# L0 prologue of a four-layer fused kernel: a new order of loads, key and value products, norms and key sums

## Chip, cores and metric

The kernel runs on 1 core of one Trainium2 chip. Time is device microseconds of one launch, median of several runs. On this core the engines work side by side: PE (TensorE: matmuls, PEld its weight loads), DVE (VectorE), ACT (ScalarE), POOL (GpSimd) and SP (SyncE, which issues the DMAs). Each takes its own list of instructions in order; semaphores tie them together.

## The reference, cut to what matters

```python
x = x + jnp.tanh(g_xattn[0]) * _L0_xattn_ref(_layernorm(x), ctx_4096, Wq, Wk, Wv, Wo)   # 16 heads of 96, 4 KV heads
x = x + jnp.tanh(g_ffn[0])   * _L0_ffn_ref(_layernorm(x), ...)                          # base + top-2 LoRA experts
x = x + jnp.tanh(g_xattn[1]) * _L1_xattn_ref(_layernorm(x), ctx_4096, ctx_4096)         # linear attention
x = x + jnp.tanh(g_ffn[1])   * _L1_ffn_ref(_layernorm(x), ...)
...                                                                                      # L2 and L3 alike, with rope
```

In L0, keys and values come from `concat([context, latents])`: `k = hidden @ Wk.T`, `v = hidden @ Wv.T`, while `q = layernorm(x) @ Wq.T`. In L1, `kh = softmax(kh, axis=1)` and `kvs = einsum('bnhd,bnhe->bhde', kh, vh)` depend on the context alone, so they can be worked out at any time: these are the "key sums". x is 8 batches of 128 tokens by 512, the context as well.

## The kernel before, in words

One core holds all of x (`x`), its normed and transposed form (`xt_hi`, `xt_lo`) and the transposed context (`ct_hi`, `ct_lo`) in SBUF. Each fp32 operand is split into a rounded part `_hi` and a rest `_lo`, and every product is a `triple` of three matmuls (lines 440 to 442). A part `_hi` is a cast on ACT; the rest is a subtraction, on DVE for what lies in PSUM and for the context, on POOL for weights.

Work on weights: SP loads a tile into one of five slots of `raw` (`load_tile`, line 458), ACT casts it (`weight_head`, L2437), POOL takes the rest (`weight_tail`, L3219) and counts `w_done` up by one. Tile n counts in its place in the list, so the waits of PE are on the number of tiles done.

The L0 attention is done in 4 groups of heads. A group's projections ("fillers") are `K`, `W` (values, before they are turned), `Q`, and `V` (the turn of `W`), the ones with n = 0 from the context (`ct_*`), those of `Q` and with n = 1 from the tokens (`xt_*`). Each takes half of the tokens: 12 matmuls of 512 columns, `V` 4 transposes. A filler is named by its place (b, k); ACT (`head`) and DVE (`evacuate`) bring its result from PSUM to SBUF. The first 11 of group 0 are the prologue; after it come `three_groups` and the rest, in an order that is written out by hand for each engine. The first work of that part is `scores(0, 0)` on PE, L2518 on ACT.

Before the 11 fillers, the kernel does eight norms one after another: DVE statistics (`norm_stats`, L1424 to L1429), POOL the power of -0.5 (`norm_rstd`, L3211), DVE the normed rows (`norm_rows`, L1437), PE four transposes (`norm_transpose`, L582), ACT the cast (`norm_head`, L2423), DVE the rest (`norm_tail`, L1451). Only then are the context's four chunks cast (ACT L3183, DVE L2398), and then the five weight tiles of group 0. ACT's first work is the tanh of the gates (L3176), which waits for their load.

The key sums are one step for each of 8 batches, `l1_keys`, dealt out one before each filler: DVE the maximum of the context rows (L1898), ACT the exponentials (L2805), PE four transposes (L975, "turn"), ACT a cast (L2813), DVE the rest (L1903), PE twelve matmuls of 128 columns ("key products"), DVE three small operations (L1908 to L1911).

SP issues the loads in this order: constants, x (8), gates and `b_thr`, the transposed context (4 of 512 KB), four weight tiles, the context rows (8), the fifth weight tile, a bias row, the output weights.

## Time and profile before

| | |
|---|---|
| median of 3 runs | 1801.08 us (1800.53 to 1801.22) |
| the profiled execution's own time | 1802.1 us |
| its span, first to last instruction | 1800.3 us |
| PE busy | 1754.0 us, 97% of the span |
| DVE, ACT, POOL busy | 1213.5, 859.0, 969.2 us |

PE is the engine that is nearly always busy. The time around the span is 1.8 us in the profiled execution. Rows of the trace give a start, a duration, the engine, the line, what is written and read, and in brackets how long the engine had been idle and what ended that.

### The profile page before, as it was taken

How to read it: one execution, taken by the hardware profiler on the slowest of the kernel's cores; microseconds unless marked ns; L12 is line 12 of the kernel's file. 1: busy time of each engine (PE TensorE's matmuls, PEld its weight loads, DVE VectorE, ACT ScalarE, POOL GpSimd, SP SyncE). 2: the span in 40 equal slices, each digit the busy share in tenths (PEclk: the TensorE clock that was granted, in tenths of full speed). 3: DMA queues.
4: the chain of work that ended last, by engine and by line, in shares of the span. 5: the costliest groups of instructions: out<-in, count | busy, mean ns of one | idle time of the engine just before them, and what ended most of it. 6: DMA issues, size and time to landing. Idle time of an engine off the chain costs nothing.

```text
span 1800.3 us, 27501 instructions
## 1 busy us (share of the span) xinstructions
PE 1754.0 (97%) x8776; PEld 1438.7 (80%) x8776; DVE 1213.5 (67%) x2204; ACT 859.0 (48%) x2451; POOL 969.2 (54%) x806
## 2 busy tenths in 40 slices
PE   4999999999999999999999999999999999999999
PEld 3788888776878888888888877878888888888887
DVE  5566566688876666666666675766666666666685
ACT  4466666553554444444444453344444444444451
POOL 3032322266575656656566563575675756757561
PEclk9999999999999999999999998999999999999999
DMA  5010100020111101101011110110110101101101
GB/s 208 6 34 21 30 24 16 21 91 12 59 42 30 47 12 52 35 29 47 17 51 36 29 34 25 41 48 19 51 35 23 47 24 46 36 22 47 31 18 48
DMA packets 36853, 69.47 MB, mean 39 GB/s; under 512 B 4362, under 2 KB 5130, under 8 KB 36658
## 3 DMA queue, kind: packets, MB, share of 16 engines
q1 hardware_dynamic: 36786, 68.61, 12.6%
q8 instruction: 37, 0.61, 0.1%
q14 instruction: 30, 0.25, 0.0%
HBM read 66.50 MB, written 2.10 MB: 38 GB/s over the span
## 4 chain that ended last, share of the span: by engine, by line
PE 91%; DVE 4%; issue 2%; ACT 2%; POOL 1%; DMA 1%; SPq 0%; POOLq 0%; ACTq 0%; DVEq 0%
PE ps L440 27%; PE ps L442 26%; PE ps L441 26%; PE ps L671 4%; PE ps L652 3%; PE ps L582 1%; PE ps L613 1%; DVE negmax L1522 1%; DMA bthr<-in_b_thr 0%; POOL probs L3268 0%; POOL rope_a L3250 0%; DVE pt_loL L1544 0%; DVE ot_lo L1555 0%; ACT probs L2518 0%; DVE ot_lo L1550 0%
## 5 line engine op out<-in xcount | busy, mean ns | idle before, releaser
L3268 POOL TENSOR_TENSOR probs<-probs,rsums 128x512 f32<-128x512 f32 (+1 forms) x160 | 194.8, 1218 | 281.4 <-DVE rsums L1540 281.2
L3250 POOL TENSOR_TENSOR rope_a<-rope_a,rope_b 128x512 f32<-128x512 f32 x160 | 206.9, 1293 | 155.0 <-DVE rope_b L1515 154.8
L440 PE MATMUL ps<-wo_hiL,ot_hi 128*128 128x512 f32 x608 | 248.8, 409 | 3.0 <-DVE ot_lo L1555 2.2
L440 PE MATMUL ps<-xt_hi,wq_hiL 128*128 128x512 f32 x608 | 242.6, 399 | 0.2
L442 PE MATMUL ps<-wo_hiL,ot_lo 128*128 128x512 f32 x608 | 241.5, 397 | 0.0
L441 PE MATMUL ps<-wo_loL,ot_hi 128*128 128x512 f32 x608 | 241.3, 397 | 0.0
L442 PE MATMUL ps<-xt_hi,wq_loL 128*128 128x512 f32 x608 | 238.0, 391 | 0.0
L441 PE MATMUL ps<-xt_lo,wq_hiL 128*128 128x512 f32 x608 | 236.9, 390 | 0.0
L2518 ACT ACTIVATE probs<-ps,negmax 128x128 f32<-128x128 f32 x512 | 182.1, 373 | 88.3 <-DVE negmax L1522 88.2
L2535 ACT CAST ot_hi<-ps 128x512 fp32r<-128x512 f32 (+1 forms) x160 | 90.7, 567 | 257.0 <-PE ps L442 256.6
L3262 POOL TENSOR_TENSOR q_loL<-rope_a,q_hiL 128x512 fp32r<-128x512 f32 x128 | 164.5, 1294 | 28.1 <-ACT q_hiL L2505 28.1
L3219 POOL TENSOR_TENSOR wq_loL<-raw,wq_hiL 128x512 fp32r<-128x512 f32 x76 | 100.0, 1317 | 125.0 <-ACT wq_hiL L2437 125.0
L1561 DVE SCALAR_TENSOR_TENSOR x<-ps,tg,x 128x512 f32<-128x512 f32 x160 | 119.0, 743 | 67.9 <-PE ps L442 66.4
L1522 DVE TENSOR_REDUCE negmax<-ps 128x4 f32<-128x512 f32 (+1 forms) x160 | 126.7, 792 | 53.2 <-PE ps L652 40.5
L1544 DVE TENSOR_TENSOR pt_loL<-ps,pt_hiL 128x512 fp32r<-128x512 f32 (+1 forms) x160 | 126.9, 793 | 41.3 <-ACT pt_hiL L2528 39.9
L2528 ACT CAST pt_hiL<-ps 128x512 fp32r<-128x512 f32 (+1 forms) x160 | 108.0, 675 | 74.7 <-PE ps L671 63.8
L440 PEld LDWEIGHTS ps<-wo_hiL,ot_hi 128*128 128x128 f32 x608 | 115.1, 189 | 33.7 <-issue 5.5
L1550 DVE TENSOR_TENSOR ot_lo<-ps,ot_hi 128x512 fp32r<-128x512 f32 (+1 forms) x160 | 105.8, 661 | 49.7 <-ACT ot_hi L2539 24.2
L442 PEld LDWEIGHTS ps<-wo_hiL,ot_lo 128*128 128x128 f32 x608 | 114.9, 189 | 27.7
L3219 POOL TENSOR_TENSOR wo_loL<-raw,wo_hiL 128x512 fp32r<-128x512 f32 x76 | 97.6, 1295 | 68.8 <-ACT wo_hiL L2437 68.7
L442 PEld LDWEIGHTS ps<-xt_hi,wq_loL 128*128 128x128 f32 x608 | 114.1, 188 | 24.8
L441 PEld LDWEIGHTS ps<-wo_loL,ot_hi 128*128 128x128 f32 x608 | 115.2, 190 | 23.3
(231 smaller groups left out, 4267.0 us busy)
## 6 DMA issues: line engine op xcount, KB each, us to landing
raw<-in_L_proj SPq DMA_DIRECT2D x108, 256.0 KB, 2.6
raw<-in_L_out SPq DMA_DIRECT2D x76, 256.0 KB, 2.6
raw<-in_F_w SPq DMA_DIRECT2D x16, 256.0 KB, 2.7
x<-in_x SPq DMA_DIRECT2D x8, 256.0 KB, 4.3
ct_raw<-in_ctx_t SPq DMA_DIRECT2D x4, 512.0 KB, 7.6
cn_raw<-in_ctx SPq DMA_DIRECT2D x8, 256.0 KB, 8.1
out<-x SPq DMA_DIRECT2D x8, 256.0 KB, 2.0
raw<-in_L_kv SPq DMA_DIRECT2D x6, 256.0 KB, 2.9
```

What stands on the lines that cost most here:

```text
L440: pe.matmul(dst, l_hi, r_hi, start=start, stop=False)
L441: pe.matmul(dst, l_hi, r_lo, start=False, stop=False)
L442: return pe.matmul(dst, l_lo, r_hi, start=False, stop=stop)
L1522: v.tensor_reduce(negmax[:, b % 2], sc, X_AXIS, ALU.max, negate=True).then_inc(L.s_smax, 1)
L1544: v.tensor_tensor(L.pt_lo[:], ps[:, T_BANK:T_BANK + L.sources, :], L.pt_hi[:], ALU.subtract).then_inc(L.s_pt, 1)
L1561: v.scalar_tensor_tensor(out=x[:, b], in0=ps[:, Y_BANK, :], scalar=tg[:, L.gate:L.gate + 1], in1=x[:, b], op0=ALU.mult, op1=ALU.add).then_ ...
L2518: e = act.activation(probs[:, row:row + L.keys], ps[:, bank + at_ // 512, at_ % 512:at_ % 512 + L.keys], ACT.Exp, bias=offset[:, b % 2, h: ...
L2528: act.copy(L.pt_hi[:], ps[:, T_BANK:T_BANK + L.sources, :]).then_inc(L.s_pt_head, 1)
L3219: gp.tensor_tensor(lo, raw[0:parts, k % RAW, 0:cols], hi, ALU.subtract).then_inc(w_done, 1)
L3250: gp.tensor_tensor(rope_a[:, a], rope_a[:, a], rope_b[:], ALU.add).then_inc(L.s_rsum, 1)
L3262: gp.tensor_tensor(lo, rope_a[:, a], hi, ALU.subtract).then_inc(L.s_qk, 1)
L3268: gp.tensor_tensor(pv, pv, rsums[:, b % 2].unsqueeze(2).to_broadcast([P, GH, L.keys]), ALU.mult).then_inc(L.s_p, 1)
```

## The change

The L0 prologue is written as one list per engine, the function `prologue(a0)` of each. The context is loaded first, in halves of four batches (`ct_in[0]`, `ct_in[1]`), and the gates last. ACT casts a half in two pieces (`context_head(0..3)`); DVE takes the rest of the first half (`ct_done`), POOL that of the second (`context_tail`, `ct_rest`). The normed rows move from DVE to ACT (`norm_rows` there, L2432, an activation with a scale and a bias), for which DVE computes a bias for each batch (`norm_shift`, L1444). The fillers come in the order PRO_TWO, weight tiles in the order K, W, Q0, Q1, Q2. The step `l1_keys` is taken apart into `key_max`, `key_exps`, `key_turn`, `key_head`, `key_tail`, `key_products` and `key_sums`, each put into the lists by itself. A filler waits for the norms of its own half only. The norms use PSUM banks 6 and 7 in place of 0 and 1. `head(7, 1)` of ACT moves from `three_groups` into the list. No work is added but the eight `norm_shift`; the context's two halves of casts are as large as the four chunks were.

```diff
@@ module level @@
+PRO_TWO = [(3, 0), (4, 1), (3, 1), (5, 0), (4, 0), (5, 1), (6, 0), (6, 1), (6, 2), (7, 0), (7, 1)]
-NORM_BANK = {"A0": 0, "F0": 0, "F1": 2, "A2": 2, "F2": 0, "A3": 2, "F3": 0}
+NORM_BANK = {"A0": 6, "F0": 0, "F1": 2, "A2": 2, "F2": 0, "A3": 2, "F3": 0}
...
-        self.prologue = PRO_ROPE if rope else [(b, k) for b in range(3, 8) for k in range(len(self.fill[b]))]
-        self.pro_weights = PRO_WEIGHTS if rope else WEIGHT_ORDER
-        self.pro_tiles = PRO_TILES if rope else list(range(self.proj_tiles))
+        self.prologue = PRO_ROPE if rope else PRO_TWO
+        self.pro_weights = PRO_WEIGHTS
+        self.pro_tiles = PRO_TILES[:self.proj_tiles]
@@ SyncE: the loads @@
             sp.dma_start(consts[:], inp["consts"]).then_inc(cst_in, 16)
-            for b in range(B):
+            def tokens(b):
                 sp.dma_start(x[:, b, :], inp["x"][b]).then_inc(x_in[b // 2], 16)
-            sp.dma_start(gates[:], inp["gates"].broadcast_to([P, 8])).then_inc(g_in, 16)
-            sp.dma_start(bthr[:], inp["b_thr"].broadcast_to([P, 1])).then_inc(g_in, 16)
-            for c in range(C):
-                sp.dma_start(ct_raw[:, c, :], inp["ctx_t"][c]).then_inc(ct_in, 16)
-            begin, groups = attention(Lq[0])
-            begin()
+            def context(c, h):
+                half = slice(h * HALF * P, (h + 1) * HALF * P)
+                sp.dma_start(ct_raw[:, c, half], inp["ctx_t"][c][:, half]).then_inc(ct_in[h], 16)
+            def context_rows(b):
+                sp.dma_start(cn_raw[:, b], inp["ctx"][b]).then_inc(cn_in[b // 4], 16)
+            def gate_rows():
+                sp.dma_start(gates[:], inp["gates"].broadcast_to([P, 8])).then_inc(g_in, 16)
+                sp.dma_start(bthr[:], inp["b_thr"].broadcast_to([P, 1])).then_inc(g_in, 16)
+            first_tile, _, groups = attention(Lq[0])
+            context(0, 0)
+            context(1, 0)
+            context(2, 0)
+            context(3, 0)
+            first_tile(0)
+            first_tile(1)
+            tokens(0)
+            tokens(1)
+            tokens(2)
+            tokens(3)
+            context_rows(0)
+            context_rows(1)
+            context_rows(2)
+            context_rows(3)
+            first_tile(2)
+            first_tile(3)
+            tokens(4)
+            tokens(5)
+            tokens(6)
+            tokens(7)
+            first_tile(4)
+            context(0, 1)
+            context(1, 1)
+            context(2, 1)
+            context(3, 1)
+            context_rows(4)
+            context_rows(5)
+            context_rows(6)
+            context_rows(7)
+            gate_rows()
@@ TensorE: fillers @@
                         if when == PROLOGUE:
                             pe.wait_ge(w_done, base + w + 1)
+                            if L.packed and (kind == "Q" or n == 1):
+                                pe.wait_ge(ln_done, HALF * (half + 1))
+                            elif L.packed:
+                                pe.wait_ge(ct_rest if half else ct_done, 2)
...
+            def key_products(b):
+                pe.wait_ge(k_done, b + 1)
+                pe.wait_ge(ct_done if b < HALF else ct_rest, 2)
...
+            def prologue(a0):
+                a0.begin(3, 0)
+                norm_transpose("A0", 0)
+                norm_transpose("A0", 1)
+                key_turn(0)
+                a0.begin(4, 1)
+                key_turn(1)
+                key_products(0)
+                key_turn(2)
+                norm_transpose("A0", 2)
+                key_products(1)
+                norm_transpose("A0", 3)
+                key_turn(3)
+                key_products(2)
+                a0.begin(3, 1)
+                key_turn(4)
+                a0.begin(5, 0)
+                key_products(3)
+                norm_transpose("A0", 4)
+                a0.begin(4, 0)
+                a0.begin(5, 1)
+                key_turn(5)
+                key_products(4)
+                norm_transpose("A0", 5)
+                norm_transpose("A0", 6)
+                key_turn(6)
+                a0.begin(6, 0)
+                norm_transpose("A0", 7)
+                a0.begin(6, 1)
+                key_products(5)
+                a0.begin(6, 2)
+                key_products(6)
+                key_turn(7)
+                a0.begin(7, 0)
+                key_products(7)
+                a0.begin(7, 1)
             pe.wait_ge(cst_in, 16)
-            for b in range(B):
-                norm_transpose("A0", b)
-            pe.wait_ge(ct_done, C)
+            a0, a2 = attention(Lq[0], "A0"), attention(Lq[1], "A2")
+            prologue(a0)
             pe.wait_ge(ln_done, B)
-            a0, a2 = attention(Lq[0], "A0"), attention(Lq[1], "A2")
-            for n, (b, k) in enumerate(Lq[0].prologue):
-                l1_keys(n)
-                a0.begin(b, k)
+            pe.wait_ge(ct_rest, 2)
             pe.wait_ge(k_sum, B)
@@ VectorE @@
+            def context_tail(p):
+                half, chunks = slice(p // 2 * HALF * P, (p // 2 + 1) * HALF * P), slice(p % 2 * 2, p % 2 * 2 + 2)
+                v.wait_ge(ct_head, p + 1)
+                v.tensor_tensor(ct_lo[:, chunks, half], ct_raw[:, chunks, half], ct_hi[:, chunks, half],
+                                ALU.subtract).then_inc(ct_done, 1)
...
+            def prologue(a0):
+                context_tail(0)
+                context_tail(1)
+                first_stats(0)
+                first_stats(1)
+                norm_shift("A0", 0)
+                norm_shift("A0", 1)
+                key_max(0)
+                first_stats(2)
+                key_max(1)
+                norm_tail("A0", 0)
+                norm_tail("A0", 1)
+                norm_shift("A0", 2)
+                key_max(2)
+                key_tail(0)
+                first_stats(3)
+                key_max(3)
+                key_tail(1)
+                norm_shift("A0", 3)
+                key_sums(0)
+                key_tail(2)
+                a0.begin(3, 0)
+                key_max(4)
+                norm_tail("A0", 2)
+                norm_tail("A0", 3)
+                key_sums(1)
+                key_sums(2)
+                first_stats(4)
+                key_tail(3)
+                key_max(5)
+                norm_shift("A0", 4)
+                a0.begin(3, 1)
+                key_sums(3)
+                first_stats(5)
+                a0.begin(5, 0)
+                norm_tail("A0", 4)
+                key_tail(4)
+                norm_shift("A0", 5)
+                key_max(6)
+                first_stats(6)
+                key_max(7)
+                norm_shift("A0", 6)
+                first_stats(7)
+                a0.begin(4, 0)
+                key_sums(4)
+                norm_shift("A0", 7)
+                norm_tail("A0", 5)
+                a0.begin(5, 1)
+                norm_tail("A0", 6)
+                key_tail(5)
+                key_tail(6)
+                norm_tail("A0", 7)
+                a0.begin(6, 1)
+                key_sums(5)
+                a0.begin(6, 2)
+                key_sums(6)
+                key_tail(7)
+                a0.begin(7, 0)
+                key_sums(7)
+                a0.begin(7, 1)
@@ ScalarE @@
-            act.wait_ge(g_in, 32)
-            act.activation(tg[:], gates[:], ACT.Tanh).then_inc(g_tanh, 1)
...
+            def prologue(a0):
+                context_head(0)
+                context_head(1)
+                a0.weights(0)
+                a0.weights(1)
+                norm_rows("A0", 0)
+                norm_rows("A0", 1)
+                key_exps(0)
+                norm_head("A0", 0)
+                norm_head("A0", 1)
+                key_exps(1)
+                key_head(0)
+                a0.weights(2)
+                key_exps(2)
+                norm_rows("A0", 2)
+                key_head(1)
+                a0.begin(3, 0)
+                key_head(2)
+                norm_rows("A0", 3)
+                key_exps(3)
+                norm_head("A0", 2)
+                norm_head("A0", 3)
+                key_head(3)
+                key_exps(4)
+                context_head(2)
+                a0.weights(3)
+                a0.begin(4, 1)
+                a0.begin(3, 1)
+                norm_rows("A0", 4)
+                key_head(4)
+                a0.begin(5, 0)
+                a0.weights(4)
+                norm_head("A0", 4)
+                key_exps(5)
+                context_head(3)
+                norm_rows("A0", 5)
+                key_exps(6)
+                a0.begin(4, 0)
+                norm_rows("A0", 6)
+                key_head(5)
+                a0.begin(5, 1)
+                norm_head("A0", 5)
+                key_head(6)
+                norm_head("A0", 6)
+                norm_rows("A0", 7)
+                gate_tanh()
+                norm_head("A0", 7)
+                key_exps(7)
+                a0.begin(6, 0)
+                a0.begin(6, 1)
+                a0.begin(6, 2)
+                key_head(7)
+                act.wait_ge(ln_t, B)
+                a0.begin(7, 0)
+                a0.begin(7, 1)
+            a0, a2 = attention(Lq[0], "A0"), attention(Lq[1], "A2")
+            prologue(a0)
@@ GpSimd @@
+            def context_tail(p):
+                half, chunks = slice(p // 2 * HALF * P, (p // 2 + 1) * HALF * P), slice(p % 2 * 2, p % 2 * 2 + 2)
+                gp.wait_ge(ct_head, p + 1)
+                gp.tensor_tensor(ct_lo[:, chunks, half], ct_raw[:, chunks, half], ct_hi[:, chunks, half],
+                                 ALU.subtract).then_inc(ct_rest, 1)
+            def prologue(a0):
+                a0.weights(0)
+                norm_rstd("A0", 0)
+                norm_rstd("A0", 1)
+                a0.weights(1)
+                norm_rstd("A0", 2)
+                a0.weights(2)
+                norm_rstd("A0", 3)
+                norm_rstd("A0", 4)
+                a0.weights(3)
+                context_tail(2)
+                norm_rstd("A0", 5)
+                context_tail(3)
+                norm_rstd("A0", 6)
+                norm_rstd("A0", 7)
+                a0.weights(4)
```

## Rows read from the trace of the kernel before

**Rows 1.** The page's head and its row of busy time.
```profile
span 1800.3 us, 27501 instructions
...
PE 1754.0 (97%) x8776; PEld 1438.7 (80%) x8776; DVE 1213.5 (67%) x2204; ACT 859.0 (48%) x2451; POOL 969.2 (54%) x806
```
**Rows 2.** Windows: us, busy time and (x instructions) of each engine, granted clock, DMA.
```profile
0.00:81.10 81.10, 53.55 (x276) 43.73 (x277) 44.93 (x96) 33.06 (x62) 13.65 (x17) 0.98 0.33 116
81.10:1800.30 1719.20, 1700.41 (x8501) 1395.00 (x8499) 1168.57 (x2108) 825.95 (x2389) 955.50 (x789) 0.99 0.12 35
```
**Rows 3.** Timeline of PE: start, us, engine, line, what, idle before.
```profile
33.66 1.09 PE L975 MATMUL ps<-consts,probs 128*128 128x128 f32 x4 [7.86 <-ACT probs L2805]
34.45 0.79 PE L440 MATMUL ps<-ct_hi,wkv_hiL 128*128 128x512 f32 x1
...
38.33 0.40 PE L440 MATMUL ps<-ct_hi,wkv_hiL 128*128 128x512 f32 x1
...
43.56 0.60 PE L975 MATMUL ps<-consts,probs 128*128 128x128 f32 x4
43.91 0.30 PE L440 MATMUL ps<-ct_hi,kt_hi 128*128 128x128 f32 x1
...
45.28 0.44 PE L440 MATMUL ps<-xt_hi,wq_hiL 128*128 128x512 f32 x1
...
75.50 0.50 PE L440 MATMUL ps<-ct_hi,wkv_hiL 128*128 128x512 f32 x1 [1.05 <-DVE q_loL L1496]
...
78.39 0.39 PE L440 MATMUL ps<-xt_hi,wq_hiL 128*128 128x512 f32 x1
...
81.11 0.28 PE L440 MATMUL ps<-k_hiL,q_hiL 96*128 96x256 f32 x1
```
**Rows 4.** Windows of the prologue around the stretch at the lower clock.
```profile
54.00:58.50 4.50, 3.31 (x28) 2.89 (x27) 3.00 (x10) 2.43 (x6) 0.00 (x0) 1.00 0.00 0
58.50:62.00 3.50, 3.50 (x14) 3.02 (x13) 2.11 (x6) 1.29 (x3) 0.00 (x0) 0.52 0.01 2
```
**Rows 5.** Waits from 33 to 81.1 us: total, times, longest.
```profile
DVE kt_lo L1903 <- ACT kt_hi L2813: 11.4, 8, 2.2
...
PE ps L440 <- DVE kt_lo L1903: 1.3, 3, 0.5
```
**Rows 6.** Timeline of SP, ACT and DVE in the first 31 us.
```profile
1.20 3.74 SPq L525 DMA_DIRECT2D x<-in_x  x8
...
12.13 0.21 ACT L3176 ACTIVATE tg<-gates 128x8 f32<-128x8 f32 x1 [10.12 <-DMA bthr<-in_b_thr]
...
26.32 3.88 ACT L3183 CAST ct_hi<-ct_raw 128x1024 fp32r<-128x1024 f32 x4
...
27.40 4.63 DVE L2398 TENSOR_TENSOR ct_lo<-ct_raw,ct_hi 128x1024 fp32r<-128x1024 f32 x4 [0.25 <-ACT ct_hi L3183]
```
**Rows 7.** Loads issued in 2.6:3.0, 4.4:4.48, 6.0:6.15, 16.4:16.5; last column: us to landing.
```profile
x<-in_x SPq DMA_DIRECT2D x1, 256.0 KB, 4.3
...
x<-in_x SPq DMA_DIRECT2D x1, 256.0 KB, 4.9
...
ct_raw<-in_ctx_t SPq DMA_DIRECT2D x1, 512.0 KB, 6.4
...
cn_raw<-in_ctx SPq DMA_DIRECT2D x1, 256.0 KB, 9.4
```
**Rows 8.** Groups by shape: busy, mean ns | idle; first to 81.1 us, others whole.
```profile
L1437 DVE TENSOR_SCALAR xn<-x,mv,rstd 128x512 f32<-128x512 f32 x8 | 4.3, 543 | 0.0
...
L2432 ACT ACTIVATE xn<-x,ve,rstd 128x512 f32<-128x512 f32 x24 | 19.6, 822 | 21.5 <-DVE ve L1444 20.8 <-PE ps L582 0.8
...
L1444 DVE TENSOR_SCALAR ve<-mv,rstd 128x1 f32<-128x1 f32 x32 | 6.4, 206 | 0.4 <-POOL rstd L3211 0.2
```
**Rows 9.** Timeline of POOL: the first two rests of weights.
```profile
30.80 2.37 POOL L3219 TENSOR_TENSOR wq_loL<-raw,wq_hiL 128x512 fp32r<-128x512 f32 x1 [6.82 <-ACT wq_hiL L2437]
33.12 1.27 POOL L3219 TENSOR_TENSOR wkv_loL<-raw,wkv_hiL 128x512 fp32r<-128x512 f32 x1
```

More of the change, by code:

```diff
@@ L98, in __init__ @@
         if self.packed:
-            for run in range(-1, groups):
+            self.order = [(-1, b, k) + self.tasks(-1, b, NOW)[k] + (0,) for b, k in self.prologue]
+            for run in range(groups):
                 for b in range(8):
@@ L379, in build @@
         x_in = [sem(f"x_in{j}") for j in range(B // 2)]
-        ct_in, ct_head, ct_done = sem("ct_in"), sem("ct_head"), sem("ct_done")
+        ct_in = [sem(f"ct_in{h}") for h in range(2)]
+        ct_head, ct_done, ct_rest = sem("ct_head"), sem("ct_done"), sem("ct_rest")
         cst_in, cst, sel_dma, sel_done = sem("cst_in"), sem("cst"), sem("sel_dma"), sem("sel_done")
@@ L470, in proj_tile, with first_tile @@
                         load_tile(base, n_static, per_loop, i, pick(wp, g, t), C * P)
+                def first_tile(n):
+                    proj_tile(L.pro_tiles[n], 0, n, 0, 0)
                 def begin():
-                    for n, t in enumerate(L.pro_tiles):
-                        if L.name == "L0" and n == L.proj_tiles - 1:
-                            for b in range(B):
-                                sp.dma_start(cn_raw[:, b], inp["ctx"][b]).then_inc(cn_in[b // 4], 16)
-                        proj_tile(t, 0, n, 0, 0)
+                    for n in range(L.proj_tiles):
+                        first_tile(n)
                 def packed_group(i):
@@ L2389, in bridge @@
                 a2.begin(7, 1)
-            v.memset(minus_half[:], -0.5).then_inc(cst, 1)
-            for s in range(B + 2):
-                if s < B:
-                    v.wait_ge(x_in[s // 2], 32)
-                norm_step("A0", s)
-            for c in range(C):
-                v.wait_ge(ct_head, c + 1)
-                v.tensor_tensor(ct_lo[:, c], ct_raw[:, c], ct_hi[:, c], ALU.subtract).then_inc(ct_done, 1)
+            def prologue(a0):
[58 more added lines that the diff above has]
+                a0.begin(7, 1)
@@ L2399, in _ @@
+            v.memset(minus_half[:], -0.5).then_inc(cst, 1)
             v.wait_ge(cst_in, 16)
-            l1_keys(0)
+            a0, a2 = attention(Lq[0], "A0"), attention(Lq[1], "A2")
+            prologue(a0)
             v.wait_ge(g_tanh, 2)
-            a0, a2 = attention(Lq[0], "A0"), attention(Lq[1], "A2")
-            for n, (b, k) in enumerate(Lq[0].prologue):
-                l1_keys(n + 1)
-                a0.begin(b, k)
             a0.groups()
@@ L2796, in turned, with context_head, gate_tanh, key_exps @@
                 act.copy(ot_hi[0:er], ps[0:er, q, :]).then_inc(f_thead, 1)
[L2798 to L2814 removed]
+            def context_head(p):
+                half, chunks = slice(p // 2 * HALF * P, (p // 2 + 1) * HALF * P), slice(p % 2 * 2, p % 2 * 2 + 2)
+                act.wait_ge(ct_in[p // 2], 64)
+                act.copy(ct_hi[:, chunks, half], ct_raw[:, chunks, half]).then_inc(ct_head, 1)
+            def gate_tanh():
+                act.wait_ge(g_in, 32)
+                act.activation(tg[:], gates[:], ACT.Tanh).then_inc(g_tanh, 1)
+                act.mul(thr[:, 3:4], bthr[:], -1.0).then_inc(g_tanh, 1)
+            def key_exps(b):
+                act.wait_ge(k_nmax, b + 1)
+                if b >= 2:
+                    act.wait_ge(k_t, b - 1)
+                act.activation(probs[:, b % 2 * D:(b % 2 + 1) * D], cn_raw[:, b], ACT.Exp,
+                               bias=negmax[:, b % 2, b // 2:b // 2 + 1],
+                               accum_out=sums[:, b % 2, b // 2:b // 2 + 1]).then_inc(k_exp, 1)
+            def key_head(b):
+                act.wait_ge(k_t, b + 1)
+                if b >= 2:
+                    act.wait_ge(k_kv, b - 1)
+                act.copy(kt_hi[:, b % 2], ps[:, 2 + b % 2, :].rearrange("p (c k) -> p c k", c=C)
+                         ).then_inc(k_head, 1)
             def table_head():
@@ L3185, in _ @@
-            for n in range(Lq[0].proj_tiles):
-                a0.weights(n)
-            l1_keys(0)
-            for n, (b, k) in enumerate(Lq[0].prologue[:-1]):
-                l1_keys(n + 1)
-                a0.begin(b, k)
+            def prologue(a0):
[53 more added lines that the diff above has]
+                a0.begin(7, 1)
@@ L3191, in _ @@
+            a0, a2 = attention(Lq[0], "A0"), attention(Lq[1], "A2")
+            prologue(a0)
+            act.wait_ge(g_tanh, 2)
             a0.groups()
@@ L3666, in bridge @@
                 a2.tail(7, 0, 0, PROLOGUE)
+            def context_tail(p):
+                half, chunks = slice(p // 2 * HALF * P, (p // 2 + 1) * HALF * P), slice(p % 2 * 2, p % 2 * 2 + 2)
+                gp.wait_ge(ct_head, p + 1)
[17 more added lines that the diff above has]
+                a0.weights(4)
             gp.wait_ge(cst, 1)
-            for b in range(B):
-                norm_rstd("A0", b)
             a0, a2 = attention(Lq[0], "A0"), attention(Lq[1], "A2")
-            for n in range(Lq[0].proj_tiles):
-                a0.weights(n)
+            prologue(a0)
             a0.groups()
```

116 lines of the change are left out of this document (39 added, 77 removed).

## The prediction, as it was put on record

> **What bounds the kernel now.** I read the page's busy times first: PE is busy for 97% of the span [rows 1]. The windows split this. From 81.1 us to the end it is busy 1700.4 of 1719.2 us; before that only 53.6 of 81.1, so 27.5 us of the 46 us that PE idles in all lie in the first 81 us [rows 2]. That boundary is `scores(0, 0)`, which starts at 81.11 [rows 3]; what comes behind it is a dense chain on PE, and a microsecond by which it starts sooner is a microsecond off the end, unless something else holds it.
>
> The timeline of PE then shows two parts. Until 33.66 PE has had 32 small transposes of the norms only; it stands 7.86 us just before the first turn of the keys, and the first filler starts at 34.45 [rows 3]. What was late: ACT stood until 12.13 for the gates, which were issued behind x; it cast the context only at 26.32 to 30.2, behind eight norms; the weight tiles follow [rows 6], and POOL takes its first rest at 30.80 [rows 9]. So nothing of the front is bound by PE, nor by bytes: it is an order.
>
> From 34.45 to 81.11 are 46.66 us. Of these, pure work at the 2.4 GHz level: nine fillers at 81.11 - 78.39 = 2.72 us (24.5), eight key products at 45.28 - 43.91 = 1.37 (11.0), seven turns at 43.91 - 43.56 = 0.35 (2.45), two V turns of as many transposes, taken the same (0.7): 38.65 [rows 3]. Two stretches ran at the 1.2 GHz level. From 34.45 to 38.33 nine matmuls took 3.88 us that at 0.227 each take 2.04: 1.8 lost, after PE had stood. In 58.5 to 62 the granted clock is 0.52, half of 3.5 us or 1.7 lost, and the 4.5 us before it had PE busy 3.31 only [rows 4]. Idle for a releaser: 1.3 behind `kt_lo` [rows 5] and 1.05 behind `q_loL` [rows 3], 2.35. The rest, 46.66 - 38.65 - 3.5 - 2.35 = 2.15, are small hesitations where one tile of work ends and another begins.
>
> **The change, part by part.** *Loads.* The first half of the context takes the places that x0 to x3 had in SP's queue, with the same size and the same 2 KB rows. SP needs 3.74 / 8 = 0.47 us for each issue [rows 6]; the fourth was issued at 2.6 and landed 4.3 later, at 6.9 [rows 7]. Weight tiles K and W take the places of x4 and x5, x0 and x1 those of x6 and x7: 4.47 + 4.9 = 9.4 [rows 6, 7]. The last context row, the 28th unit of 256 KB, was in issue at 16.4 and landed 9.4 us after its issue had begun, at some 25.5 [rows 7]; from x7 on that is 20 units in 16 us, with the gates' small packets between. At 0.65 to 0.79 a unit the rows of batches 0 to 3 land at 13.5 to 15, the second half of the context at 20 to 23, rows 4 to 7 at 23 to 26. The gates, the bias and the output weights come behind these; nobody waits for them before 60 us.
>
> *The first filler.* Context at 6.9; two casts at 3.88 / 4 = 0.97 [rows 6] to 8.9; DVE's two rests at 4.63 / 4 = 1.16 [rows 6] from 7.9 to 10.3; the K tile's cast ends at 9.5. POOL's rest took 2.37 the first time and 1.27 the second [rows 9]; the 2.37 began at 30.80 while DVE was in its last `ct_lo`, which ended at 32.03 [rows 6], 1.1 us before it. From 10.3 with 1.27 it ends at 11.6, and with 2.37 from 9.5 at 11.9. I take 11.6 for the first filler, 22.85 us sooner than before.
> The Trainium skill, "SBUF — State Buffer", section "Who interferes with whom", says that a DVE instruction with two SBUF inputs and a GpSimd one that reads SBUF exclude each other. By this rule the first rest waits for DVE to 10.3 in this order too; without it K would start at 10.8, and the sum would be 0.8 us lower. The row's 2.37 beside 1.27 agrees with the rule but is the first of its kind too, so it cannot prove it.
>
> *PE's work from there.* As before plus eight norm transposes and the first turn: nine more at 0.35, 3.15, so 41.8 us. The transposes had been in the idle front; now they count.
>
> *DVE.* Busy 44.9 us up to 81.1 before [rows 2]; half of the context's rests go to POOL (-2.3), the normed rows to ACT (-4.3), eight shifts come (+1.6), the last Q with its two rests (+1.3) now counts: 41.2 [rows 8]. It starts at 7.9, so it cannot end before 49.
> *ACT.* 33.1, plus 8 x 0.82 of normed rows [rows 8], plus the last Q's two casts 1.1: 40.8, from 6.9 on: about 47 at the least. *POOL.* 13.7 plus two halves of `ct_lo`; POOL's price for 1024 columns is not in a row as such, two of 1.27 make 2.5 and two of 2.37 make 4.7: 19 to 23, no bound. So PE remains the longest, by 4 us over DVE: both lists have to mesh nearly without a gap.
>
> *Walking the four lists* with these durations, a cast 0.6, a rest 0.65, a reduction 0.6, statistics 1.0, key sums 0.86, each from the earliest time at which all its waits are met: K from 11.6 to 16; transposes and the first turn to 17.2; W to 20; small pieces to 26, bound by the ring of exponentials, turn, cast, rest; DVE reaches `key_max(4)` at 24.3, and if the rows land at 26 it stands there with `norm_tail` 2 and 3 behind it, for which Q0 waits. Q0 at 26.3; Q1 at 31.85, held by Q0's rest; K1 to 37.4; W1 at 40.8, held by Q1's rest; Q2 at 43.9; the second half's K at 50, Q0 at 54.1. POOL has both rests of the context at 37.3, `key_products(4)` wants them at 37.7. In this walk PE stands 1.8 us in all. The new waits (norms by halves, `ct_done`, `ct_rest`) are met before PE comes, except the one for Q0 (0.35, in the 1.8).
>
> *The sum.* 11.6 + 41.8 of work + 1.8 for the start at the lower level, as before + 2.1 of hesitations, as before + 1.8 of waits + 1.7 for one more stretch at the lower level = 60.8 us for `scores(0, 0)`, 20.3 sooner. I count the last term since the stretch from 20 to 26 holds the same mix as 54 to 58.5 did, small matmuls with gaps [rows 4]. The profiled execution was 1802.1, 1.0 above the median of 1801.08; 1801.1 - 20.3 = **1780.8 us**. Behind 81.1 nothing changes: the parity of banks is the same after 11 fillers, and POOL, DVE and ACT had been idle at that point.
>
> **Where a rule speaks against it.** PE now starts 23 us sooner but with small, broken work between the fillers. The row: PE lost half its rate for 3.5 us behind a broken stretch, though it never stood for more than 0.6 us at once there [rows 4]. The Trainium skill, "TensorE: Matmul & The Clock Gate", section "What's actually happening", says that the throttled level is the default and activity releases it. By the rule alone, without the row's count, the whole small-piece part from 16 to 26 might stay at 1.2 GHz, 5 us lost in place of 1.7; the sum would be 64.
>
> **The rivals.**
> A. *The lists mesh worse: DVE waits for ACT as before.* DVE stood 11.4 us in eight waits for the keys' cast, 1.4 each [rows 5]. If half of that stays in a list that has 4 us of room, little is lost; if all stays, DVE ends at 49 + 11.4 = 60.5 plus its waits for loads and fillers, and `scores` comes at 64 to 69: 1785 to 1789. For it: both lists are over 90% full. Against: keys are now dealt out where something else lies between, and the 11.4 were idle time in a list with nothing else to do.
> B. *The loads come late.* The bytes ahead of x0 are as before, but the first 512 KB piece behind the gates took 6.4 us and landed at 12.5 [rows 7]. If context and weights share the engines so that all come at 11 to 12, K starts at 16: 1785.
> C. *The clock.* A microsecond at 1.2 GHz costs half a microsecond. 15 us more of it give +7.5: 1788. The gain is gone when 41 us more of the prologue run there; at the lower level throughout, the end is 11.6 + 2 x 41.8 + 3.9 = 99, 18 later than now: 1819, **slower**. Against: dense fillers lie in between, and at 38.3 the level rose after 3.9 us of them [rows 3].
> D. *All goes well:* no second stretch, waits under 1 us: 58 to 59, 1778.
> E. *Given back later.* DVE and ACT come to `scores(0, 0)` later than before against PE, or the low stretches fall otherwise: some 2 us either way. That the whole gain is taken up later would need an engine other than PE as the bound behind 81 us; its idle time there is 18.8 of 1719 us [rows 2].
>
> **How the numbers follow.** Forecast with its own spread (1777 to 1784): 0.55. D 0.10 (some of it below 1777), A 0.16, B 0.07, C partly 0.08, C wholly or an unforeseen stall that takes all 0.02, the rest 0.02 no change. So faster by over 0.2% (3.6 us, what a measurement here can tell) 0.96, same 0.02, slower 0.02. The range takes in D and E below and A, B and part of C above: 1774 to 1790.
>
> **What would show it.** In the changed profile: first filler at 11.6 (10.8 to 14); ACT's first cast at 6.9; `scores(0, 0)` at 58 to 64; DVE busy over 85% from 10 us to there; a granted clock of about 0.5 in one stretch of 3.5 us; from there on the same distance to the end as before, 1719.2 us, within 2. It is wrong if DVE's idle time in the prologue is above 10 us, if the clock is low in several stretches, or if that distance has grown.

## The result, and the profile after

The changed kernel takes 1777.43 us (median of 4 runs, 1777.12 to 1779.62) beside 1800.8 us before (1800.49 to 1801.22): a ratio of 0.9872 with a 95% interval from 0.9857 to 0.9886, 1.3% faster, 23.4 us. The forecast was 1780.8 us, with a range of 1774 to 1790. The profiled execution took 1779.62 us, with a span of 1777.8.

The page's head and its row of busy time, as in [rows 1]:

```profile
span 1777.8 us, 27517 instructions
...
PE 1747.3 (98%) x8776; PEld 1435.8 (81%) x8776; DVE 1208.9 (68%) x2202; ACT 864.3 (49%) x2459; POOL 972.0 (55%) x808
```

PE has as many instructions as before and 6.7 us less busy time, though no matmul was removed. Up to `scores(0, 0)` it is 8.0 us less (53.55 before [rows 2], 45.54 now). The 32 norm transposes alone account for 4.25 of that: they were busy for 8.83 us where they came in small groups with PE standing between them, and for 4.58 us among the fillers. The stretch at a granted clock of 0.52 [rows 4] is gone as well. The windows, cut at `scores(0, 0)` as in [rows 2], then from the first filler to it, then the densest part:

```profile
0.00:58.04 58.04, 45.54 (x276) 39.92 (x277) 39.28 (x94) 38.12 (x70) 16.24 (x19) 1.00 0.46 161
58.04:1777.80 1719.76, 1701.74 (x8501) 1395.84 (x8499) 1169.61 (x2108) 826.16 (x2389) 955.73 (x789) 0.99 0.12 35
12.45:58.04 45.59, 45.54 (x276) 39.88 (x277) 35.70 (x88) 33.81 (x65) 14.04 (x14) 1.00 0.36 128
18.00:46.00 28.00, 27.95 (x182) 24.63 (x181) 26.32 (x64) 26.07 (x52) 11.28 (x10) 1.00 0.38 131
```

`scores(0, 0)` comes at 58.04 in place of 81.11, 23.07 us sooner; behind it lie 1719.76 us where [rows 2] has 1719.20. The whole gain is ahead of that point, and it reaches the end. From the first filler to there PE is busy 45.54 of 45.59 us, at a granted clock of 1.00. The last row shows how dense the other engines' lists have become: from 18 to 46 us DVE is busy for 26.3 of 28 us and ACT for 26.1.

The timeline of the first filler on PE and what came before it, from the lists of PE, ACT, DVE and POOL, as in [rows 3, 6, 9]:

```profile
12.45 0.77 PE L443 MATMUL ps<-ct_hi,wkv_hiL 128*128 128x512 f32 x1 [12.45 <-POOL wkv_loL L3393]
...
16.37 0.40 PE L443 MATMUL ps<-ct_hi,wkv_hiL 128*128 128x512 f32 x1
...
17.07 1.03 PE L622 MATMUL ps<-consts,xn 128*128 128x128 f32 x8
```

```profile
7.79 1.99 ACT L2925 CAST ct_hi<-ct_raw 128x1024 fp32r<-128x1024 f32 x2 [5.64 <-DMA ct_raw<-in_ctx_t]
```

```profile
8.86 2.36 DVE L1537 TENSOR_TENSOR ct_lo<-ct_raw,ct_hi 128x1024 fp32r<-128x1024 f32 x2 [8.00 <-ACT ct_hi L2925]
...
49.15 0.69 DVE L1570 TENSOR_TENSOR q_loL<-ps,q_hiL 96x512 fp32r<-96x512 f32 x1 [2.64 <-ACT q_hiL L2615]
```

```profile
10.45 1.90 POOL L3393 TENSOR_TENSOR wkv_loL<-raw,wkv_hiL 128x512 fp32r<-128x512 f32 x1 [10.01 <-ACT wkv_hiL L2562]
```

The first half of the context lands at 7.79; two casts follow, two rests on DVE to 11.22, the K tile's rest on POOL to 12.35, and PE starts at 12.45. Its first nine matmuls take 3.92 us, 12.45 to 16.37, or 0.43 each; the ones after them are 0.23 apart. That is the 1.2 GHz level, after PE had stood from the start of the kernel. It is read from this spacing only: the column of the granted clock has 1.00 for this stretch too. DVE's row at 49.15 shows that it has caught up by then: it waits for ACT's cast of a filler that has only just ended. POOL's row gives the price that the prediction could only bound:

```profile
31.90 2.38 POOL L3845 TENSOR_TENSOR ct_lo<-ct_raw,ct_hi 128x1024 fp32r<-128x1024 f32 x1
```

### The profile page after: what moved, and what is told of

Same layout as the page of the kernel before. It is cut to its first block, busy times and chain, and to the rows that moved or that the text cites. A ratio compares the mean times of both kernels' runs of the same rounds, so it can differ in the third digit from the quotient of the medians.

```text
span 1777.8 us, 27517 instructions
## 1 busy us (share of the span) xinstructions
PE 1747.3 (98%) x8776; PEld 1435.8 (81%) x8776; DVE 1208.9 (68%) x2202; ACT 864.3 (49%) x2459; POOL 972.0 (55%) x808
## 4 chain that ended last, share of the span: by engine, by line
PE 92%; DVE 3%; issue 2%; POOL 1%; ACT 1%; DMA 0%; SPq 0%; POOLq 0%; DVEq 0%; ACTq 0%
PE ps L443 27%; PE ps L445 27%; PE ps L444 27%; PE ps L715 4%; PE ps L696 3%; PE ps L622 1%; PE ps L653 1%; DVE negmax L1598 1%; POOL probs L3442 0%; DVE ot_lo L1631 0%; POOL rope_a L3424 0%; DVE pt_loL L1620 0%; DVE ot_lo L1626 0%; DMA ct_raw<-in_ctx_t 0%; PE ps L1080 0%
## 5 line engine op out<-in xcount | busy, mean ns | idle before, releaser
L443 PE MATMUL ps<-ct_hi,wkv_hiL 128*128 128x512 f32 x304 | 122.9, 404 | 12.4 <-POOL wkv_loL L3393 12.4
L445 PEld LDWEIGHTS ps<-xt_hi,wq_loL 128*128 128x128 f32 x608 | 114.1, 188 | 24.5
```

Of the source, the lines that this page charges most:

```text
L443: pe.matmul(dst, l_hi, r_hi, start=start, stop=False)
L445: return pe.matmul(dst, l_lo, r_hi, start=False, stop=stop)
```

## The experiments

For each, with its median and the two times that the trace gives for PE: where the first filler starts and where `scores(0, 0)` does. "Between" is the time from the one to the other, "behind" the span less the latter. Medians lie up to 3.3 us off the profiled execution, so starts are compared by the traces. The kernel before, run beside the others, had medians of 1800.3 to 1801.1.

| kernel | first filler | scores(0, 0) | between | behind | median us |
|---|---|---|---|---|---|
| before | 34.45 | 81.11 | 46.66 | 1719.2 | 1801.08 |
| changed | 12.45 | 58.04 | 45.59 | 1719.8 | 1777.43 |
| changed, again | 12.37 | 57.99 | 45.62 | 1717.3 | 1778.08 |
| e1 before, gates last | 30.85 | 77.60 | 46.75 | 1719.3 | 1798.60 |
| e2 old loads | 19.55 | 65.23 | 45.68 | 1717.7 | 1784.85 |
| e3 four norms first | 25.13 | 69.98 | 44.85 | 1718.9 | 1790.64 |
| e10 whole context first | 18.61 | 64.34 | 45.73 | 1719.8 | 1785.49 |
| e4 rows on DVE | 12.79 | 61.82 | 49.03 | 1717.3 | 1780.70 |
| e6 rests on DVE | 12.99 | 60.91 | 47.92 | 1717.4 | 1779.72 |
| e5 keys one a filler | 12.18 | 77.73 | 65.55 | 1717.9 | 1797.43 |
| e7 transposes first | 12.73 | 60.42 | 47.69 | 1717.6 | 1778.29 |
| e8 K tile first | 12.50 | 58.21 | 45.71 | 1717.4 | 1777.44 |
| e9 transposes and K tile first | 12.54 | 60.63 | 48.09 | 1719.6 | 1778.75 |
| e11 transposes, rows sooner | 13.04 | 56.97 | 43.93 | 1717.9 | 1776.63 |

**Does TensorE's start set the end?** Four kernels are built to move the start. The first changes the kernel before:

```diff
-            sp.dma_start(gates[:], ...); sp.dma_start(bthr[:], ...)      # behind x
...
             begin()
+            sp.dma_start(gates[:], ...); sp.dma_start(bthr[:], ...)
...
-            act.wait_ge(g_in, 32)                                        # tanh: ACT's first work
...
+            act.wait_ge(g_in, 32)                                        # behind ACT's prologue
```

> The kernel before with one thing moved: the loads of the gates behind the weights, and the tanh behind ScalarE's prologue. Theory that the 4.07 us for which VectorE stood at 9.0 to 13.08 lay on the path: the norms, casts and first filler all come 3.5 to 4 us sooner, 1797. Rival, that the context's load (landed at 17.2) or another list bound it anyway: no change, 1801.

1798.60 (1795.37 to 1800.89, 10 runs), a ratio of 0.9985 with an interval from 0.9976 to 0.9995. In its trace ACT's first cast of a norm comes at 8.86 in place of 12.46, the first filler 3.60 and `scores(0, 0)` 3.51 sooner than before. So the gates' wait held the kernel before by 3.5 us; the median shows 2.5 of it against the kernel before run beside it (1801.09).

```diff
@@ SyncE: e2, loads in the old order, lists as changed @@
+            tokens(0) ... tokens(7)
+            gate_rows()
+            context(0, 0) ... context(3, 0), context(0, 1) ... context(3, 1)
+            first_tile(0) ... first_tile(3)
+            context_rows(0) ... context_rows(7)
+            first_tile(4)
```

> The changed kernel's lists with the loads in the old order (x, gates, context, four weights, context rows, last weight). The K tile lands at some 18 in place of 8. Theory that the first filler's start sets the end since TensorE never waits after it: first filler at 19.9, everything 7.5 to 8.5 later, 1785.5. Rival, that the order of work in the lists is what brings the gain and the loads have room: under 3 us lost, 1778 to 1780.

1784.85 (1784.52 to 1785.44), 7.4 above the changed kernel, at the lower edge of what was expected. The first filler is 7.10 later, `scores(0, 0)` 7.19: the lists keep their 45.7 us whatever the start. The other 15.9 us of the gain stay with the old order of loads, so they come from the lists. No run takes the lists apart further than e3 to e6 and e10 do.

```diff
@@ e3: all four lists, here PE's @@
+                norm_transpose("A0", 0)
+                norm_transpose("A0", 1)
+                norm_transpose("A0", 2)
+                norm_transpose("A0", 3)
                 a0.begin(3, 0)
-                norm_transpose("A0", 0)
-                norm_transpose("A0", 1)
```

> The changed kernel with the norms of batches 0 to 3 ahead of the context's casts and the K product, in all four lists; loads as in the changed kernel. First filler at some 21. Theory that TensorE's start sets the end: 8.7 later, less four norm transposes that now lie ahead of it (1.4), 1784.5. Rival, that VectorE's list (41 us of work) sets the end and its work is only in another order: 1 to 2 us, 1779.

1790.64 (1789.85 to 1790.80), 13.2 above the changed kernel. The start came at 25.13, 4 us later than I had worked out: DVE's fourth `norm_tail` ended at 21.3, not 17.5, the norms being a ring over four engines of some 2 us a turn that nothing else fills. With it `scores(0, 0)` moved by 11.9: 12.7 of start, less the four transposes that no longer lie between (0.35 each, 1.4), within 0.7. The rule held, my time for four norms did not. Four norms ahead of the first filler thus cost more than the old loads did. But not all of the 12.7 us are norms: e3 keeps the new loads, in which x comes behind the context, and DVE stood until 10.03 for it.

```diff
@@ e10: the context whole, all rests on DVE @@
+            context(0, 0), context(0, 1), context(1, 0) ... context(3, 1)
             first_tile(0)
...
+                act.wait_ge(ct_in[0], 64)
+                act.wait_ge(ct_in[1], 64)
...
+                context_head(0) ... context_head(3)      # ACT; DVE has context_tail(0) ... context_tail(3)
                 a0.weights(0)
```

> The changed kernel with the context loaded and cast whole, ahead of everything, its rests all on VectorE: both halves land before the first cast. Four more loads of 0.65 us and two more casts and rests come before the first filler: it starts at 15.7 in place of 12.45. Theory that the start sets the end: 3.3 us later, 1780.7. Rival, that the lists get the work back, since all of it has to be done anyway: under 1 us, 1778.

1785.49 (1784.40 to 1785.97). The start moved by 6.16, not 3.3, and `scores(0, 0)` by 6.30, so the rule held again and my start did not. The lists of ACT, DVE and POOL give the parts:

```profile
10.38 1.28 ACT L2928 ACT_TABLE_LOAD   x1 [10.38 <-DMA ct_raw<-in_ctx_t]
11.68 3.88 ACT L2928 CAST ct_hi<-ct_raw 128x1024 fp32r<-128x1024 f32 x4
```

```profile
12.75 4.63 DVE L1537 TENSOR_TENSOR ct_lo<-ct_raw,ct_hi 128x1024 fp32r<-128x1024 f32 x4 [11.90 <-ACT ct_hi L2928]
```

```profile
16.23 2.28 POOL L3396 TENSOR_TENSOR wkv_loL<-raw,wkv_hiL 128x512 fp32r<-128x512 f32 x1 [15.79 <-ACT wkv_hiL L2564]
```

The last of the eight loads landed 2.59 us later than the fourth had (10.38 for 7.79). Here ACT's table load comes only then and not at 0.86, which puts the first cast 1.30 later; it is the one kernel with two waits ahead of ACT's first instruction. From the first cast to the end of DVE's last `ct_lo`, at 17.38, are 5.70 us in place of 3.43, 2.27 more. That makes 6.16. Of these my 3.3 had the loads (2.6) and 0.7 for the rest. POOL's rest begins at 16.23 and ends at 18.51, 1.13 us after DVE's last `ct_lo`. In the changed kernel it ends 1.13 after it too, so this is no part of the difference.

**Is TensorE alone the bound, or VectorE with it?** Two kernels give DVE work back:

```diff
@@ e4, VectorE: and norm_rows leaves ACT's list @@
-                norm_shift("A0", b)
+                norm_rows("A0", b)
```

> The changed kernel with the normed rows back on VectorE (norm_rows in the place of norm_shift) and off ScalarE. VectorE gets 4.3 - 1.6 = 2.7 us more, ScalarE 6.6 less. Theory that TensorE alone binds and the lists have room: 0 to 1 us, 1777.4 to 1778.4. Rival, that VectorE is as much a bound: 2.7 to 3.5 us later, 1780 to 1781.

```diff
@@ e6, VectorE: and context_tail leaves POOL's list @@
                 norm_shift("A0", 4)
+                context_tail(2)
                 a0.begin(3, 1)
...
+                context_tail(3)
                 key_max(6)
```

> The changed kernel with the rests of the context's second half on VectorE in place of GpSimd (2.38 us there, 1.16 on VectorE). VectorE gets 2.3 us more. Theory that TensorE alone binds: 0 to 0.5, 1777.4 to 1778. Rival, that VectorE binds too: 2.3 later, 1779.7.

e4: 1780.70 (1780.23 to 1781.95), 3.3 above the changed kernel. e6: 1779.72 (1778.86 to 1780.52), 2.3 above; its runs touch those of the changed kernel (1777.05 to 1779.62 in both sets), so I go by its trace. From the first filler to `scores(0, 0)` e4 took 3.44 us more and e6 2.33. The waits of PE in e4 and, below, in e6, over that stretch:

```profile
PE ps L443 <- DVE q_loL L1572: 1.8, 2, 1.2
PE ps L443 <- DVE xt_lo L1526: 0.5, 1, 0.5
```

```profile
PE ps L443 <- DVE q_loL L1572: 1.6, 2, 1.3
```

So the rival was right: DVE has no room in this part, and most of what is given to it comes out at the end. e4 also took 5.5 us from ACT in this stretch (33.81 to 28.29) and was slower all the same, so ACT is not the tighter of the two. PE's busy row of 97% and more does not show that a second engine is as tight.

The sizes fit less well than they look. I had priced DVE's added work at 2.7 us in e4 and at 2.3 in e6. In e4 three of the eight normed rows took 1.05 to 1.70 us in place of 0.54, each while POOL was in a subtraction, and each ended 0.28 or 0.29 us after it. DVE's list, then POOL's:

```profile
38.63 1.70 DVE L1512 TENSOR_SCALAR xn<-x,mv,rstd 128x512 f32<-128x512 f32 x1
```

```profile
37.65 2.40 POOL L3837 TENSOR_TENSOR ct_lo<-ct_raw,ct_hi 128x1024 fp32r<-128x1024 f32 x1
```

The eight rows cost DVE 7.0 us, 5.3 more than the eight shifts (1.7), so e4's 3.44 us are for 5.3 added. In e6 one of the two rests took 1.73 beside POOL's rest of a weight, so its 2.33 are for 2.9. Where in DVE's list the added work stands was not varied.

**Does the order of the key sums matter?** e5 keeps all work, loads and engines and deals the key sums out one batch before each filler, with the norm transposes spread to suit; PE's list, with DVE's and ACT's changed to match:

```diff
                 a0.begin(4, 1)
+                norm_transpose("A0", 2)
                 key_turn(1)
                 key_products(0)
-                key_turn(2)
-                norm_transpose("A0", 2)
-                key_products(1)
                 norm_transpose("A0", 3)
-                key_turn(3)
-                key_products(2)
                 a0.begin(3, 1)
+                key_turn(2)
+                key_products(1)
+                a0.begin(5, 0)
...
```

> The changed kernel with the key sums dealt out evenly, one batch before each filler, in place of three turns and products between the W and the first Q product. Theory that this early block is what fills TensorE's time until four norms are done: Q waits at 24 for norms that come at 26, TensorE stands 2 us or more in all, and the broken stretch may bring the lower clock level (1.7 more): 1779.5 to 1781.5. Rival, that the place of the key sums does not matter: 1777.4.

1797.43 (1795.86 to 1798.56, 10 runs), a ratio to the kernel before of 0.9981 (0.9971 to 0.9990): 20 of the 23.4 us are gone, five to ten times what I had expected. The waits of PE, then six windows and the whole stretch:

```profile
PE ps L1015 <- ACT probs L2936: 4.1, 2, 2.1
...
PE ps L443 <- DVE k_loL L1566: 3.4, 1, 3.4
...
PE ps L443 <- DVE kt_lo L1976: 1.5, 2, 1.3
```

```profile
24.00:28.00 4.00, 0.59 (x5) 0.36 (x4) 2.81 (x6) 3.94 (x9) 0.00 (x0) 0.91 0.58 212
28.00:32.00 4.00, 4.00 (x13) 3.11 (x14) 2.30 (x7) 1.53 (x3) 1.81 (x2) 0.67 0.00 0
...
40.00:44.00 4.00, 2.02 (x19) 1.78 (x17) 3.24 (x7) 3.62 (x8) 0.00 (x0) 1.00 0.00 0
44.00:48.00 4.00, 4.00 (x14) 3.17 (x13) 2.06 (x6) 0.76 (x2) 2.88 (x2) 0.57 0.00 0
48.00:52.00 4.00, 1.88 (x11) 1.31 (x10) 2.67 (x6) 3.08 (x7) 0.00 (x0) 0.89 0.01 2
52.00:56.00 4.00, 4.00 (x18) 3.81 (x17) 1.84 (x5) 1.36 (x3) 1.69 (x2) 0.50 0.00 0
```

```profile
12.18:77.73 65.55, 56.47 (x277) 47.29 (x277) 36.78 (x88) 34.49 (x65) 13.99 (x14) 0.84 0.26 91
```

PE stood 9.0 us for these three, and each standing is followed by a stretch at the lower level: 0.16 of 65.55 is 10.5 us lost to the clock. 9.0 + 10.5 = 19.5, against the 19.96 by which the stretch is longer. A wait of a microsecond on PE thus cost two here. Not every wait does: in e4 and e6 PE waited for 2.6 and 1.8 us in all, up to 1.3 at once, and the granted clock stayed at 1.00. One thing is my own doing: the first Q waited 3.4 us for `k_loL`, which frees its PSUM bank, since I had put K's rest behind two norm tails in DVE's list and K's cast behind a norm's in ACT's. So the run shows that another order of the same work can lose nearly all; it does not show that dealing the key sums out evenly must.

**Can the low level at the start be had away?** PE stands until 12.45; e7 gives it something to do:

```diff
             pe.wait_ge(cst_in, 16)
+            for r in range(64):
+                pe.transpose(ps[:, 5, r % C * P:(r % C + 1) * P], ident, ident)
```

> The changed kernel once more, as the measure for the three that run with it. Both theories: 1777.4 us, 23.4 below the kernel before.

> 64 transposes of the identity on TensorE before its first filler, into a PSUM bank that is free then; in the changed kernel nine matmuls of the first filler ran 0.43 us apart. Theory that the lower level there comes only from the engine having stood: the first filler runs 0.23 us apart from its start, scores(0, 0) 1.9 us sooner, 1775.5. Rival, that small transposes don't raise the level (they did not in the kernel before, where they came in groups with gaps): no change, or later by what the transposes delay, 1777.4 to 1779.

1778.29 (1776.40 to 1781.09) beside 1778.08 for the changed kernel timed with it (1777.05 to 1779.22): no difference. In PE's list the transposes do what they are for, and DVE's list shows what takes the gain in the profiled execution:

```profile
2.96 10.01 PE L1466 MATMUL ps<-consts 128*128 128x128 f32 x64 [2.96 <-DMA consts<-in_consts]
12.73 0.48 PE L443 MATMUL ps<-ct_hi,wkv_hiL 128*128 128x512 f32 x1
13.04 0.40 PE L444 MATMUL ps<-ct_lo,wkv_hiL 128*128 128x512 f32 x1
...
28.25 0.47 PE L443 MATMUL ps<-xt_hi,wq_hiL 128*128 128x512 f32 x1 [2.22 <-DVE xt_lo L1528]
```

```profile
26.23 0.69 DVE L1973 TENSOR_REDUCE negmax<-cn_raw 128x1 f32<-128x512 f32 x1 [2.29 <-DMA cn_raw<-in_ctx]
```

```profile
27.00:31.00 4.00, 2.75 (x9) 2.21 (x10) 3.79 (x12) 3.38 (x6) 0.07 (x1) 0.78 0.02 8
31.00:35.00 4.00, 4.00 (x27) 3.50 (x26) 2.07 (x5) 2.09 (x4) 4.00 (x3) 0.80 0.22 66
```

The first filler takes 2.8 us in place of 4.6. Then DVE comes to `key_max(4)` at 23.9, before the rows of the context have landed, and stands until 26.23 with `norm_tail` 2 and 3 behind it. PE stands 2.22 for those, and the clock takes another 0.22 x 4 + 0.20 x 4 = 1.7. This is more than the 1.8 gained: `scores(0, 0)` comes 2.4 later than in the changed kernel. The spread of the five times, 1776.40 to 1781.09, suggests that not every execution lost so much. In the changed kernel DVE comes there at 25.34, and the rows had landed at 24.5. In e7 and e9 they land at 26.2 and 26.4, in the seven kernels that load them at the same place and have no transposes (changed, changed again, e3 to e6, e8) at 24.2 to 25.2; no run shows why.

e8 loads and casts the K tile ahead of the context; e9 has both edits.

```diff
+            first_tile(0)
             context(0, 0)
...
+                a0.weights(0)
                 context_head(0)
```

> The K tile is loaded and cast ahead of the context. In the changed kernel its rest ran on GpSimd from 10.45 to 12.35, and the first matmul waited for it. Theory that this rest sets TensorE's start and that every microsecond of the start reaches the end: the start is then set by VectorE's rests of the context, which come some 0.5 later than now (11.7), so 0.7 us sooner, 1776.7. Rival, that the lists of VectorE and ScalarE bind as much as TensorE: no change.

> Both edits: the K tile first and 64 transposes of the identity. If both theories hold and TensorE alone binds the prologue, 2.6 us sooner than the changed kernel, 1774.8. Rival: ScalarE and VectorE, over 90% busy from 18 to 46 us in the changed kernel, can't follow, and TensorE waits for them: 1776 to 1777.4.

e8: 1777.44 (1777.30 to 1779.44), no change. K's rest is done by 5.81, but the context, one load behind, lands 1.1 later, and PE starts at 12.50 on DVE's `ct_lo`. The first cast of the context waits for its fourth piece, and what is put ahead of it makes it later. The rest of K took 1.26 us here, though it was POOL's first of its kind:

```profile
4.55 1.26 POOL L3393 TENSOR_TENSOR wkv_loL<-raw,wkv_hiL 128x512 fp32r<-128x512 f32 x1 [4.11 <-ACT wkv_hiL L2562]
```

e9: 1778.75 (1777.85 to 1782.02), above both of its theories, with a PE wait of 1.9 us for `xt_lo` and a granted clock of 0.96 in the stretch, as in e7.

From this follows a version that should keep the 1.8 us: 60 transposes, and the rows of batches 4 to 7 loaded sooner.

```diff
             first_tile(2)
-            first_tile(3)
+            context_rows(4) ... context_rows(7)
+            context(0, 1) ... context(3, 1)
             tokens(4)
             tokens(5)
+            first_tile(3)
             tokens(6)
             tokens(7)
             first_tile(4)
-            context(0, 1) ... context(3, 1)
-            context_rows(4) ... context_rows(7)
```

> 60 transposes ahead of the first filler, as in the run with 64, and the context rows of batches 4 to 7 loaded right after the third weight tile, ahead of the second context half and the tokens of batches 4 to 7. With the transposes alone the first filler took 2.8 in place of 4.6 us, but VectorE then stood 2.29 us for these rows, which landed at 26.2, TensorE stood 2.22 behind it, and the lower level came for a while. Theory that these rows' landing is the only thing that took the 1.8 us back: VectorE does not stand there, no lower level, scores(0, 0) at 56.3, 1.7 sooner than in the changed kernel, about 1775.7. Rival, that VectorE's and ScalarE's lists hold the pace by then: TensorE stands elsewhere and scores(0, 0) comes at 57.5 to 58.5, 1777.4.

1776.63 (1776.14 to 1777.80), `scores(0, 0)` at 56.97, between the two theories. DVE no longer stands for the rows, no window of the prologue has a clock under 1.00, and the stretch from the first filler is 43.93, 1.66 shorter than in the changed kernel. But the first filler started at 13.04, since the first half of the context landed at 8.42 in this execution (7.5 to 8.3 in the others that load it first):

```profile
13.04 0.50 PE L443 MATMUL ps<-ct_hi,wkv_hiL 128*128 128x512 f32 x1 [0.40 <-POOL wkv_loL L3395]
```

So the place of the loss in e7 is shown. That the version is faster than the changed kernel is not: 0.8 us lower in the median, not timed beside it, with ranges that overlap.

## Why the prediction was right, step by step

**The path.** That `scores(0, 0)` is the point to look at and that a microsecond there is one at the end held in all fourteen traces: behind it come 1717.3 to 1719.8 us. These fall into two groups, around 1717.6 and 1719.5. In the one pair that I looked into, the difference is mostly the clock in a later layer: in the changed kernel's two profiled executions the window from 420 to 430 has a granted clock of 0.66 in the one of 1719.8 and of 0.83 in the one of 1717.3, which is 1.7 us of the 2.5 between them.

**The first filler:** 11.6 predicted, 12.45 measured. The context landed at 7.79 and not at 6.9, the only part that was off; casts, rests and the blocked rest on POOL came as worked out. The Trainium skill's rule that the two instructions exclude each other ("SBUF — State Buffer", section "Who interferes with whom") was left open by the one row of before. Now there are three more: 1.90 and 2.28 us where DVE had two SBUF inputs, each ending 1.13 after it, and 1.26 in e8, the first of its kind, with DVE idle. The trace agrees with the rule and not with a cost of the first call.

**The work:** 45.59 us less 1.9 for the low start leaves 43.7; against 41.8 of work that is 1.9 of hesitations, where the sum had 2.1. PE's part of the sum was right to 0.2 us; the other lists were priced too heavy: DVE was busy for 39.3 us up to `scores(0, 0)`, ACT for 38.1 and POOL for 16.2, where 41.2, 40.8 and 19 to 23 were forecast.

**Two terms were too large:** the waits (1.8) and the second stretch at the lower level (1.7). Neither came: no releaser shows on PE after 12.45, and the granted clock is 1.00. This is the 2.8 us between 60.8 and 58.04: -1.8, -1.7, -0.2 for hesitations, +0.1 for the low start, +0.85 for the first filler. So the forecast of 1780.8 came as near as it did partly by luck: the late loads hid some of what the two terms had added. The two are one here: no standing, no fall of the clock. I had put the second stretch down to the mix of small matmuls; the same mix from 21 to 27 us without gaps stayed at 2.4 GHz (granted clock 1.00). The falls in e5 and e7 each come behind PE's standing, though in e4 and e6 PE stood too and the clock did not fall.

**The rivals.** A, DVE waiting for ACT: its wait for the keys' cast is gone (11.4 before [rows 5]), so it did not come about, but the reason given for it, that both lists are over 90% full, is true in 18 to 46 us, and e4 and e6 show what it costs to overfill one. DVE's share from 10 us on was forecast above 85% up to `scores(0, 0)`; it was 78% from the first filler (35.70 of 45.59), since it is full only to 46. DVE's idle time from its first `ct_lo` to `scores(0, 0)` was 9.96 us, and above 10 was to show that the prediction is wrong: a badly chosen sign, since 5.9 us of this idle time are behind 46, and PE waited for nothing. B came in small, 0.9 us. C, the clock, did not come about in the changed kernel; e5 shows what it would have cost, with 10.5 us lost, or 21 us at the lower level, and another 9.0 of waits. It stayed on the faster side of the kernel before, as it should while less than 41 us more run at the lower level. D, to which I gave 0.10, is what happened: 58 to 59, and no second stretch. E, the part behind, differed by 2.5 us between two executions of one and the same kernel.

**Where the 23.07 us came from.** The first filler starts 22.0 sooner; between it and `scores(0, 0)` lie 3.15 more of work (norm transposes and the first turn) and 4.2 less of waits and low clock. Of what sets the start, three parts were taken by themselves: 3.5 for the gates in the kernel before (e1), 7.1 for the order of loads (e2), 12.7 for four norms with their wait for x (e3). These overlap and cannot be added.

## What to carry to other kernels

Look at the front of a kernel whose main engine is 97% busy: what stood there was paid in full, and here it was an order of work and not its amount. Find the first work whose inputs come soonest and let the rest be dealt out behind it. When lists are made to mesh, sum each engine's work over the dense part. Here the second engine was busy for 94% of it (26.3 of 28 us), and most of what was added to it came out at the end. Take the price of added work from the trace that has it: DVE's normed rows cost 0.54 us alone and up to 1.70 beside POOL. On TensorE a wait can cost twice, once standing and once in the lower clock behind it (9.0 and 10.5 us in e5, 2.2 and 1.7 in e7, though nothing more in e4 and e6), so an order that leaves gaps can lose most of what a sooner start has won.

## What the runs showed of the hardware

- Transposes of the identity, 60 to 64 back to back while TensorE had nothing else to do, brought its next filler to 0.23 us a matmul from the second on. Without them its first nine ran 0.43 apart. The granted clock of the profile does not show this low start.
- ScalarE's table load (1.28 us) came at 10.38 in the one kernel with two waits ahead of ScalarE's first instruction (e10), as the last of the loads landed. It came at 0.7 to 0.9 in all the others, which have one. Two waits as the cause rest on this one kernel.
- GpSimd's subtraction with both inputs in SBUF does not run beside VectorE's: 1.90 and 2.28 us against 1.26 alone. The other way round VectorE is held: its normed rows took 1.05 to 1.70 us against 0.54 alone, and ended 0.28 or 0.29 us after GpSimd's subtraction (e4).
